# One graph layer with expert network on one core: comparison arrays built a step ahead, gathers released in fours by the experts' quarters, attention sums rebuilt with a joined mask and halving adds

## The reference

```
msg  = relu(xn[src] + edge_attr @ We + be)               # per edge
aggr = segment_sum(msg, dst); z = xn + aggr              # GINE
gnn  = layernorm(relu(relu(z @ W1 + b1) @ W2 + b2) + xn)
mix  = linear attention block and MLP of xn
x    = x + gnn + mix
y    = layernorm(x)
h    = y @ W_gat                                         # 16 columns = 4 heads x 4 experts
e    = leaky_relu(a_src[src] + a_dst[dst])               # edges and a loop per node
agg  = segment_sum(h[src] * softmax over dst of e) + b_gat
s    = layernorm(agg).reshape(4 heads, 4 experts).mean(heads)
g    = softmax of the two best of s, 0 for the others
out  = x + sum over experts of g_i * (gelu(y @ W1_i + b1_i) @ W2_i + b2_i)
```

## Time and profile before

| | us |
|---|---|
| median of 3 runs | 3788.47 (3782.95 to 3798.07) |
| the profiled execution's own time | 3779.81 |
| its span, first to last instruction | 3777.8 |

### The profile page before, as it was taken

The page is one execution under the profiler, slowest core; times in us unless marked ns, Lnnn a source line. Parts: engine busy times, 40 slices in busy tenths (PEclk is TensorE's granted clock), DMA queues, the critical chain, the costliest instruction groups (busy, mean ns, idle before and its releaser), DMA issues. The chain is left out here.

```text
span 3777.8 us, 34904 instructions
## 1 busy us (share of the span) xinstructions
PE 2708.7 (72%) x10528; PEld 1927.9 (51%) x10528; DVE 1621.8 (43%) x3135; ACT 692.7 (18%) x1082; POOL 1704.2 (45%) x1746
## 2 busy tenths in 40 slices
PE   3887888788788777799998865766766766765007
PEld 2666666666666655666665542433434433434006
DVE  6444555455454467666778960000000000001784
ACT  1111111111111123223332220111101101101005
POOL 1565656556565510022221216666666666662211
PEclk8777777777777779999999986878878877877558
DMA  7433333333333332200000013222222212213415
GB/s 259 131 105 91 106 101 106 99 100 104 97 108 93 99 99 74 68 23 23 23 23 12 9 12 70 37 36 37 37 36 37 37 31 37 41 30 109 145 59 229
DMA packets 215309, 280.82 MB, mean 74 GB/s; under 512 B 95634, under 2 KB 166312, under 8 KB 213706
## 3 DMA queue, kind: packets, MB, share of 16 engines
q0 software_dynamic: 68416, 133.35, 14.6%
q1 hardware_dynamic: 105994, 108.62, 9.3%
q10 hardware_dynamic: 40832, 38.01, 3.2%
HBM read 215.36 MB, written 64.48 MB: 74 GB/s over the span
## 5 line engine op out<-in xcount | busy, mean ns | idle before, releaser
L421 POOL DMA_INDIRECT xg<-xn_dram,gidx x784 | 743.9, 949 | 526.2 <-DVE gidx L562 283.2
L1962 POOL DMA_INDIRECT er<-row_dram,gi x784 | 739.9, 944 | 430.7 <-issue 411.9
L2023 PE MATMUL ps_en<-ew,hid 128*128 128x256 f32 x1568 | 404.5, 404 | 216.6 <-issue 213.4
L2095 DVE TENSOR_TENSOR eo<-ps_en,eb_r 128x1024 f32<-128x1024 f32 (+1 forms) x52 | 60.5, 1163 | 1157.7 <-remote 851.5
L2013 PE MATMUL ps_em<-zT_all,ew 128*128 (+2 forms) x832 | 420.4, 646 | 190.9 <-issue 123.7
L456 PE MATMUL ps_e<-we,eaT 65*128 65x256 f32 x1568 | 507.2, 480 | 69.3 <-issue 56.2
L473 PE MATMUL ps_a<-arena 128*128 128x256 f32 x1568 | 522.1, 491 | 34.6 <-ACT arena L506 26.4
L2023 PEld LDWEIGHTS ps_en<-ew,hid 128*128 128x128 f32 x1568 | 314.7, 202 | 311.6 <-issue 271.6
L473 PEld LDWEIGHTS ps_a<-arena 128*128 128x128 f32 x1568 | 399.0, 256 | 134.2 <-ACT arena L506 34.8
L456 PEld LDWEIGHTS ps_e<-we,eaT 65*128 65x128 f32 x1568 | 356.8, 239 | 138.8 <-issue 74.0
L2013 PEld LDWEIGHTS ps_em<-zT_all,ew 128*128 128x128 f32 x832 | 172.9, 215 | 419.6 <-issue 386.8
(11 more groups left out here) (291 smaller groups left out, 2877.0 us busy)
## 6 DMA issues: line engine op xcount, KB each, us to landing
eaT<-in_eaT SPq DMA_DIRECT2D x98, 256.0 KB
eo_dram<-eo ACTq DMA_DIRECT2D x48, 512.0 KB
eo<-eo_dram SPq DMA_DIRECT2D x12, 2048.0 KB
xg<-xn_dram,gidx POOLq DMA_INDIRECT x784
er<-row_dram,gi POOLq DMA_INDIRECT x784
xm<-xm_dram SPq DMA_DIRECT2D x24, 512.0 KB
erow<-arena ACTq DMA_DIRECT2D x1, 10240.0 KB
erow<-er SPq DMA_DIRECT2D x196, 40.0 KB
```

The lines of the kernel that those rows point to most:

```text
L421: pool.indirect_dma_start(xg[:, q, b, :], None, M["xn_dram"], bass.IndirectOffsetOnAxis(ap=gidx[:, q, b:b + 1], axis=0)).then_inc(s_g[q][b ...
L1962: pool.indirect_dma_start(er[:, r, b, :], None, M["row_dram"], bass.IndirectOffsetOnAxis(ap=gi[:, r, b:b + 1], axis=0)).then_inc(s_get[r], 16)
L2023: m = pe.matmul(ps_n[b][:, t, :], hid[:, b, c, t * P:(t + 1) * P], w2[:, e, c, :], start=(c == 0), stop=(c == KE - 1))
```

## The change

In `gine_windows` DVE's three comparisons of step k+1 are issued after the messages and `gidx` of step k and before the wait for its zT add. The first comparisons stand ahead of the loop, and the last two steps stand behind it.

In `nodes_and_order` the number of rounds is at least 1.

In `gat_edges_and_experts` POOL waits before every 4 gathers rather than every 16; the count comes from ACT, one after each of a unit's four Gelus, with a start of 8. DVE no longer counts.

In `attend_and_combine`: no iota and no copy `at`; `starti` is made first and used directly as the offsets; 32 small memsets make `slotf`. The mask and the destination's term are joined once, in `shift` (128 x 6272), so each group has one add less. `pr` has two buffers with 33 slots of 20 columns: 16 weighted values and 4 weights, ACT writing the exponents straight into it. The sums over slots, of weights and values together, are five adds that halve the slots (32 to 16, 8, 4, 2, 1) and one more with the scaled former sums (slot 32). The sums of group i-1 are done between the scores and the weighting of group i. The hardware loops over groups are written out in full. The prefetch of the experts' outputs is in 16 pieces of 512 KB, each released after a group of the attention, for EB = 4 buffers. In the final normalisation, the multiplication by r and the addition of the bias are made after the mean over heads, on 196 columns instead of 784.

```diff
 gine_windows, DVE
+                def compare(k, q, n):
+                    dve.wait_ge(s_am[q], n + q)
+                    nc.vector.tensor_tensor(inwin[:, q, :, :], ..., ALU.is_equal).then_inc(s_win[q], 1)
+                    dve.wait_ge(s_cnt[q], n)
+                    nc.vector.tensor_tensor(hot_hi[:, q, :, :], ..., ALU.is_equal).then_inc(s_hi, 1)
+                    nc.vector.tensor_tensor(hot_lo[:, q, :, :], ..., ALU.is_equal).then_inc(s_hot, 1)
+                def step(i, q, more):
+                    k = 2 * i + q
+                    for h in range(2):
+                        dve.wait_ge(s_e[q], i * 2 + (h + 1))
+                        dve.wait_ge(s_g[q][h], i * 64 + 64)
+                        nc.vector.tensor_tensor(msg[:, q, h * HB:(h + 1) * HB, :]..., ps_e[h][:, :], xg[...], ALU.add).then_inc(s_sum, 1)
+                    dve.wait_ge(s_sum, 2 * k + 2)
+                    stage_next(i, q)
+                    if more:
+                        compare(k + 1, 1 - q, i + q)
+                    dve.wait_ge(s_nt, k + 1)
+                    dve.wait_ge(s_agg, k)
+                    add_window(bass.ds(k, 1), 1 - q)
...
+                compare(0, 0, 0)
+                with dve.Fori(0, LASTI) as i:
                     for q in range(2):
+                        step(i, q, True)
+                step(LASTI, 0, True)
+                step(LASTI, 1, False)
 gat_edges_and_experts
-        AHEAD = 4
+        AHEAD = 8
                 with pool.Fori(0, last) as j:
-                    pool.wait_ge(s_pace, j + 1)
-                    pool.sem_inc(s_go, 1)
                     for r in range(R):
+                        pool.wait_ge(s_pace, j * R + (r + 1))
+                        pool.sem_inc(s_go, 1)
                         gather(j, r)
 ACT, rise, after each Gelu
+                        act.sem_inc(s_pace, 1)
+                act.sem_inc(s_pace, AHEAD)
+                act.sem_inc(s_pace, E2 // (P * MB))
 DVE, give
-                    dve.sem_inc(s_pace, 1)
-                dve.sem_inc(s_pace, AHEAD)
 attend_and_combine
-    EB = 5
+    EB = 4
+                for i in range(EB):
+                    for x in range(NE):
+                        n = 1 + (i * NE + x) * (NG - 2) // (EB * NE)
+                        sp.wait_ge(s_read[n % 2], n // 2 + 2)
+                        sp.dma_start(eo[:, i, :, x, :], M["eo_dram"][:, i * G:i * G + G, x, :]).then_inc(s_eo[i], 16)
...
+                        act.wait_ge(s_sum, turn * (NG + 1) + max(i, 1))
+                        nc.scalar.activation(pr[:, i % 2, 0:T, :, HC:ROWC], e[:, 0:T, :, :], ACT.Exp).then_inc(s_exp, 1)
...
-                nc.gpsimd.iota(slot[:, :], pattern=[[1, K]], base=0, channel_multiplier=0).then_inc(s_iota, 1)
-                        nc.gpsimd.tensor_copy(at[:, b, 0:T], starti[...]).then_inc(s_at, 1)
...
+                def add_up(i, T, s, turn):
+                    b = i % 2
+                    here = slice(i * G, i * G + T)
+                    dve.wait_ge(s_read[b], turn * USES[b] + (i // 2 + 2))
+                    w = K // 2
+                    while w:
+                        s.last()
+                        s.done(nc.vector.tensor_tensor(pr[:, b, 0:T, 0:w, :], pr[:, b, 0:T, 0:w, :], pr[:, b, 0:T, w:2 * w, :], ALU.add))
+                        w //= 2
+                    s.last()
+                    nc.vector.tensor_tensor(sums[:, here, :], pr[:, b, 0:T, 0, :], pr[:, b, 0:T, K, :], ALU.add).then_inc(s_sum, 1)
...
+                    for i, T in groups():
+                        scores(i, T, s, turn)
+                        if i:
+                            add_up(i - 1, G, s, turn)
+                        weigh(i, T, s, turn)
+                    add_up(NG, 1, s, turn)
```

More of the change, by code:

```diff
@@ L2276, in _, with begin @@
                 a = M["rows"][:, :, 0:HEADS]
+                c.done(nc.vector.tensor_copy(start[:, :], M["off"][:, 0:NT]))
+                c.done(nc.vector.tensor_copy(left[:, :], M["deg"][:, 0:NT]))
+                for b in range(2):
+                    dve.sem_inc(s_read[b], 1)
+                dve.sem_inc(s_sum, 1)
+                c.last()
+                def begin(turn):
+                    nc.vector.tensor_scalar(starti[:, :], start[:, :], float(ROWC), None, ALU.mult).then_inc(s_round, 1)
@@ new lines, in shifts @@
+                def shifts(s):
+                    s.done(nc.vector.tensor_tensor(mask[:, :, :], slotf[:, None, :].broadcast_to([P, NT, K]), left[:, :, None].broadcast_to([P, NT, K]), ALU.is_ge))
+                    s.last()
+                    s.done(nc.vector.tensor_scalar(mask[:, :, :], mask[:, :, :], PAD, None, ALU.mult))
+                    s.last()
+                    s.done(nc.vector.tensor_tensor(shift[:, :, :, :], mask[:, :, :, None].broadcast_to([P, NT, K, HEADS]),
+                                                   M["adst"][:, :, None, :].broadcast_to([P, NT, K, HEADS]), ALU.add))
@@ new lines, in weigh @@
+                def weigh(i, T, s, turn):
+                    b = i % 2
+                    here = slice(i * G, i * G + T)
+                    dve.wait_ge(s_exp, turn * (NG + 1) + (i + 2))
+                    for t in range(T):
+                        x = nc.vector.tensor_tensor(pr[:, b, t, 0:K, 0:HC].rearrange("p k (h c) -> p k h c", c=NE),
+                                                    el[:, b, t, :].rearrange("p (k c) -> p k c", c=ROWC)[:, :, HEADS:].rearrange("p k (h c) -> p k h c", c=NE),
+                                                    pr[:, b, t, 0:K, HC:ROWC, None].broadcast_to([P, K, HEADS, NE]), ALU.mult)
+                        if t < T - 1:
+                            s.done(x)
+                    x.then_inc(s_read[b], 1)
+                    scale = pr[:, b, 0:T, K, HC:ROWC]
+                    s.done(nc.vector.tensor_tensor(pr[:, b, 0:T, K, 0:HC].rearrange("p t (h c) -> p t h c", c=NE),
+                                                   sums[:, here, 0:HC].rearrange("p t (h c) -> p t h c", c=NE),
+                                                   scale[:, :, :, None].broadcast_to([P, T, HEADS, NE]), ALU.mult))
+                    s.last()
+                    s.done(nc.vector.tensor_tensor(scale, scale, sums[:, here, HC:ROWC], ALU.mult))
@@ new lines, in _ @@
+                begin(0)
+                c.done(nc.vector.tensor_tensor(den[:, :, :], a, M["adst"][:, :, :], ALU.add))
+                for k in range(K):
+                    c.done(nc.vector.memset(slotf[:, k:k + 1], float(k)))
+                c.done(nc.vector.tensor_tensor(end[:, :], M["off"][:, 0:NT], M["deg"][:, 0:NT], ALU.add))
+                c.done(nc.vector.tensor_copy(sums[:, :, 0:HC], M["rows"][:, :, HEADS:ROWC]))
+                c.done(nc.vector.memset(sums[:, :, HC:ROWC], 1.0))
@@ L2277, in _ @@
+                c.last()
+                c.done(nc.vector.scalar_tensor_tensor(m[:, :, :], den[:, :, :], 0.2, den[:, :, :], ALU.mult, ALU.max))
                 for x in range(NE):
@@ L2353, in _ @@
-                    over_groups(dve, group)
-                c.done(nc.vector.tensor_scalar(den[:, :, :], den[:, :, :], 1e-16, None, ALU.add))
+                    for i, T in groups():
+                        scores(i, T, s, turn)
[3 more added lines that the diff above has]
+                    add_up(NG, 1, s, turn)
+                    dve.wait_ge(s_sum, turn * (NG + 1) + (NG + 2))
+                    begin(turn + 1)
@@ L2356, in _ @@
+                    s.end(True)
+                c.done(nc.vector.tensor_scalar(den[:, :, :], sums[:, :, HC:ROWC], 1e-16, None, ALU.add))
                 c.last()
@@ L2366, in rowwise @@
                     c.last()
+                c.done(nc.vector.tensor_reduce(fbm[:, :], fb[:, :].rearrange("p (h c) -> p c h", c=NE), AX.X, ALU.add))
                 rowwise(agg, bgat[:, None, :].broadcast_to([P, NT, HC]), ALU.add)
```

196 lines of the change are left out of this document (71 added, 125 removed).

## The result

The changed kernel takes 3866.74 us (median, 3862.47 to 3883.33) where the kernel before takes 3791.55: ratio 1.0202, 95% interval 1.0166 to 1.0237, so 75 us slower (63 to 90 by the interval; whether it is more than 2% these runs don't settle). The profiled execution took 3883.33 us, its span is 3881.6 us, 103.8 more than before.

What follows compares the result with a forecast made beforehand. No engine was full; PE's signals late in gather bursts were taken as held until the burst's end. From the profiled 3779.8 us, +164 + 0 - 16 - 27 = +121 gave 3901, as median 3910 us; likeliest range 3815 to 4100.

Steps and rivals of the forecast that it cites:

- the likeliest case: Whole kernel: joined bursts make the GINE step 13.6 to 17 us; range 3815 to 4100 us, chance 0.50.
- Part 1: GINE loop, comparisons a step ahead: bursts join to 16, step 14.6 us in place of 12.93, +164 us (+36 to +400).
- above 283 and 7 us: GINE loop, signs of a right forecast: POOL's `gidx` idle grows above 283 us, pauses of 7 us and more.
- stage 1 lasts 1370 us or more: Sign of a right forecast for the GINE window loop, which had lasted from 100 to 1367 us.
- Rival A: GINE loop: PE's signals pass or its work ends before the hold; 10.7 to 11.5 us a step, 3565 us; chance 0.33.
- rival B: GINE loop: long bursts come, but only comparisons made them dear; 13.3 to 13.5 us a step, 3790 us; chance 0.12.
- 10.7 per step, PE's own time: GINE loop: step time without any hold-back, from PE's busy 1046 us over 98 steps; -218 us.
- Part 2: Experts' stage, credits of four gathers from ACT after each Gelu: taken as 0, ends -60 and +98 us.
- Part 3: Head of the attention: no iota or copy, big loads held back, scoring starts earlier; -16 us (-10 to -17).
- Part 4: Attention loop: group 11.0 us in place of 13.3, twelve groups; -27 us (-34 to -15).
- Part 5: Scores and combine: 196-wide operations -1 us, EB 5 to 4 +1 us, at most +3; together 0.

Runs made afterwards that it cites:

- e2: The changed kernel with the experts' stage pacing of the kernel before (16 gathers per bias add of DVE, lead 64): 3794.53 us, ratio 1.0013.
- e1: The changed kernel with the GINE loop of the kernel before (comparisons just ahead of their own step's messages): 3796.54 us, ratio 1.0009.
- e11: The changed kernel with four gathered blocks a step in place of eight in the GINE loop, rows half missing: 3262.71 us, ratio 0.8601.
- e4: The changed kernel with two plain transfers of fixed rows per GINE step in place of eight indirect gathers, rows wrong: 3260.05 us, ratio 0.8599.
- e6: The changed kernel with AHEAD 16 in place of 8 (lead of 64 gathers), credits of four still from ACT: 3879.4 us, ratio 1.0239.
- e7: The changed kernel with credits given by DVE, four at a time right after its bias add, lead still 32: 3793.19 us, ratio 0.9996.
- e8: The changed kernel with the one joined add into `shift` cut into 13 adds by group: 3858.82 us, ratio 1.0166.
- e10: The changed kernel with e8's attention, former pacing, and each GINE gather batch waiting for PE's sums of two steps before: 3683.16 us, ratio 0.9701.
- e12: As e10, but POOL's wait for the sums stands between the fourth and fifth gather of a batch: 3648.92 us, ratio 0.9617.

## Why the prediction came out as it did

The time, 3867, lies in the likeliest case's own range (3815 to 4100), and the direction is that of the forecast. Two of the terms were off, in opposite directions, and that the sum fits is luck in good part. The forecast rested on part 1 alone for the loss, and part 1 doesn't outweigh the attention's gain: with the former pacing (e2) the kernel takes 3794.53 us, ratio 1.0013. Nor does the pacing by itself (e1, 1.0009). It takes both to make the kernel slower, and one of them was put at 0. (A small slip besides: the chance of "faster by more" is 0.33 + 0.17 / 3 = 0.39 and not 0.37.)

- **Part 1.** The mechanism is what happened: bursts of sixteen in nearly every pair, and the low end I had worked out for the pair, 27.6 us, is the measured 27.66. POOL waits 374 us for `gidx`, mostly in pauses of 7.9 us; above 283 and 7 us were my signs. The sign "stage 1 lasts 1370 us or more" did not come: the loop is 1336 us, 13.6 a step, the very edge of the forecast's 13.6 to 17. The mis-sized term is the choice of 14.6 us per step, "near the middle of 13.8 and 15.55": PE did not fill what the comparisons left. +76 was measured where I took +164. Rival A failed (e11 shows what it would have needed), rival B named this price, but as less likely; I should have believed the sum from the rows and not widened it upward. One reading of the earlier trace rows was wrong as well: nsum doesn't wait for the transposes but for the sums (L473), and these ended at 984.97 in that burst, just ahead of nsum at 985.00. There PE itself was late, as in the changed kernel above, and no signal of the sums was held:

```profile
983.47 1.50 PE L473 MATMUL ps_a<-arena 128*128 128x256 f32 x2 [1.03 <-issue]
985.00 0.38 ACT L498 ACTIVATE nsum<-ps_a 128x256 f32<-128x256 f32 x1 [13.89 <-PE ps_a L473]
```

- The floor "10.7 per step, PE's own time" was wrong. PE's busy time of before contained its lower clock, and without long runs the step is 7.5 us (e4, e11). The floor that was left is POOL's, 10.0 us. A busy time measured in a stage that waits is no floor for that stage.
- **Part 2.** I took 0 and gave +98 as the end "if each of 49 units waited 2 us more". This is what came, +72 in the two traces. The step that failed: "finer credits come in the same places". They come behind ACT's store and first Gelu (e6, e7). I had the row of ACT's Gelu, 1.92 us after the bias add, and did not add it.
- **Part 3.** -14.7 against -16, but by two errors that cancel. POOL starts gathering 4.5 us after the last bias add (3631.19 against 3626.7), 5.9 earlier than the iota had (3481.00 against 3470.6), and then is locked out for 6 us. I had weighed the rule on the shared port only for the comparisons, and read it wrongly there. The Trainium skill ("SBUF — State Buffer", SBUF: two separate sides) names as holders of the port that DVE and GpSimd share a DVE operation in a 2-port mode, or one with two SBUF inputs, the latter only against a GpSimd operation that reads SBUF. The comparisons have one input in PSUM and are no such case, so their gathers of 0.95 us don't speak against it. The add into `shift` has two inputs in SBUF: the 7.13 us gather beside the 6.69 us add, and the 1.12 us one of e8, agree.
- **Part 4.** -36 in the loop where I took -27. The sum of the rows was 10.65 us per group, the measured one is 10.25; the 11.0 that I took for "strided columns" was a surcharge without a row. The halving adds are within 0.05 us of the estimate. El was never late.
- **Part 5.** Right: -1.6 for the scores, and 84.6 us against 84.7 for the combine.
- **Spread.** Over the profiled executions (e4 left aside), the GINE loop with the old order takes 1261, 1276 and 1299 us, with the new one 1316 to 1336 (five); the experts' stage with DVE as giver 1190 to 1217 (six), with ACT as giver 1243 to 1276 (seven). So the parts are worth about +48 and +55 in the mean, and the two profiled executions happened to show more of both. With -52 for the attention this gives +51, which is under the 63 to 90 us that were measured; by the times of e1 and e2 the parts are worth 70 and 72 us. What makes the difference of some 20 us is not shown: one profiled execution tells such a stage only to 20 to 40 us.

## What to carry to other kernels

When the releaser of the largest wait is "remote", look what another engine was doing all through that wait; here a long run of indirect gathers delayed what PE had long done. So ask of an edit that takes work off the path whether it lets such a run grow: here it did, and cost more than it gave. Where an engine's start can't be timed by position in program order, tie it to the signal that must get through (e10, e12). Before moving a credit to another engine, count what that engine has queued ahead of it.

## What the runs showed of the hardware

- What PE signals late in an unbroken run of gathers is seen only after it: no delay with runs of 4 (4.7 us; e11), 1.66 us after the end of 8 (median of the kernel before 1.68), 3.85 us after 16.
- In the later part of a run of 16 gathers PE issues its products singly, eight in 9.2 us in place of 1.89, without a wait that the profile shows (after, 293.36 to 302.57).
- With such waits gone PE's granted clock in the GINE loop was 1.00 and not 0.77, and two PE groups that took 491 and 477 ns a product before take 380 and 384 (L473 and L456, in e4 L472 and L455).
- A gather of 0.95 us took 7.13 us beside one DVE add with both inputs in SBUF, and 0.946 us on average beside comparisons with one input in PSUM (274 gathers of the kernel before).
- The same stage differs from execution to execution by 2 to 3% (the GINE loop with the old order 1261 to 1299 us, in three kernels); the whole of the kernel before took 3759.66 to 3825.56 us over all executions on record, 1.7%.
